# Three pairs of chunks added on VectorE ahead of the head sums in an edge-wise graph attention, with small copies moved to ScalarE

## The reference

```
def gatv2_layer(x, Ws, bs, Wd, bd, attn, src, dst):
    hs = (x @ Ws + bs).reshape(N, H, HD)              # N 1250, H 8, HD 96
    hd = (x @ Wd + bd).reshape(N, H, HD)
    hs_e = hs[src]                                    # one row per edge, sorted by dst
    e = jax.nn.leaky_relu(hs_e + hd[dst], SLOPE)
    logits = jnp.einsum('ehd,hd->eh', e, attn)        # 8 logits per edge
    m = jax.ops.segment_max(logits, dst, num_segments=N)
    ex = jnp.exp(logits - m[dst])
    s = jax.ops.segment_sum(ex, dst, num_segments=N)
    alpha = ex / s[dst]
    out = jax.ops.segment_sum(alpha[..., None] * hs_e, dst, num_segments=N)
    return jax.nn.elu(out).reshape(N, DM)
x = x + gnn(layernorm(x)) + linear_attention(layernorm(x))
x = x + ffn(layernorm(x))
```

## Time and profile before

| what | kernel before |
|---|---|
| time of three executions | 2284.72 us (2283.73 to 2286.36) |
| span of the profiled execution, first to last instruction | 2282.6 us |
| PE busy | 2141.9 us, 94% |
| DVE busy | 1671.1 us, 73% |
| ACT busy | 1120.7 us, 49% |
| POOL busy | 770.2 us, 34% |
| mean granted clock of TensorE | 0.974 of full speed |
| HBM traffic | 169 GB/s over the span |

### The profile page before, as it was taken

One profiled execution on the slowest core, in us unless ns is written; L12 is line 12 of the kernel. 1 busy time (PEld: TensorE's weight loads), 2 busy tenths in 40 slices (PEclk: granted clock), 3 DMA queues, 4 the chain that ended last, 5 costly groups with the idle time before them and its releaser, 6 DMA issues. The chain is left out here.

```text
span 2282.6 us, 91572 instructions
## 1 busy us (share of the span) xinstructions
PE 2141.9 (94%) x32341; PEld 1718.3 (75%) x32342; DVE 1671.1 (73%) x4413; ACT 1120.7 (49%) x2757; POOL 770.2 (34%) x798
## 2 busy tenths in 40 slices
PE   5999999998999999999996899899999999999578
PEld 3665555555899999999995556589999999999467
DVE  5224997343888888888887674488888888888873
ACT  1101210023666666666664324466666666666463
POOL 0000001111555555555552001255555555554000
PEclk9999999999999999999998899999999999999789
DMA  5000224333788888888874024488888888887301
GB/s 190 0 1 11 76 97 101 106 121 86 239 251 250 252 250 248 247 256 252 251 249 135 23 85 131 131 244 252 251 249 252 251 252 251 250 249 225 133 22 47
DMA packets 139236, 397.61 MB, mean 174 GB/s; under 512 B 21704, under 2 KB 76267, under 8 KB 139123
## 3 DMA queue, kind: packets, MB, share of 16 engines
q0 software_dynamic: 59584, 298.64, 43.0%
q1 hardware_dynamic: 76525, 90.41, 12.6%
q10 hardware_dynamic: 3044, 7.45, 1.1%
HBM read 368.18 MB, written 16.78 MB: 169 GB/s over the span
## 5 line engine op out<-in xcount | busy, mean ns | idle before, releaser
L498 ACT ACTIVATE at_relu<-at_turned,ah_attn_size 128x512 f32<-128x512 f32 x1092 | 717.9, 694 | 432.0 <-PE at_turned L557 430.6
L479 POOL DMA_INDIRECT at_rows<-table,ah_index x360 | 361.3, 1004 | 295.3 <-DVE ah_index L681 104.1
L479 POOL DMA_INDIRECT ah_room<-table,ah_index x352 | 351.5, 998 | 291.1 <-DVE ah_index L681 122.4
L555 PE MATMUL at_turned<-ah_place,dst_rows 96*128 96x128 bf16 x2208 | 401.1, 223 | 19.3 <-ACTq L533 9.6
L557 PE MATMUL at_turned<-ident,ah_room 128*128 128x128 f32 x2208 | 416.4, 279 | 0.0
L557 PE MATMUL at_turned<-ident,at_rows 128*128 128x128 f32 x2160 | 403.6, 277 | 0.5 <-issue 0.4
L555 PE MATMUL at_turned<-at_place,dst_rows 96*128 96x128 bf16 x2160 | 388.9, 222 | 0.0
L677 DVE SCALAR_TENSOR_TENSOR sums<-sums,at_factor,at_total 128x97 f32 x1456 | 344.0, 310 | 9.0 <-issue 5.1
L557 PEld LDWEIGHTS at_turned<-ident,ah_room 128*128 128x128 f32 x2208 | 317.7, 144 | 24.8
L557 PEld LDWEIGHTS at_turned<-ident,at_rows 128*128 128x128 f32 x2160 | 308.0, 143 | 23.2 <-issue 0.6
L667 DVE TENSOR_TENSOR at_spread<-at_lined,at_weight 128x1024 f32<-128x1024 f32 x182 | 223.0, 1225 | 131.4 <-ACT at_weight L508 118.0
(11 more groups left out here) (318 smaller groups left out, 3195.8 us busy)
## 6 DMA issues: line engine op xcount, KB each, us to landing
at_flags<-run_flags SPq DMA_DIRECT2D x182, 64.0 KB
dst_rows<-pr_parts SPq DMA_DIRECT2D x76, 144.0 KB, 2.5
ah_place<-local_rows SPq DMA_DIRECT2D x92, 96.0 KB
at_place<-local_rows SPq DMA_DIRECT2D x90, 96.0 KB
table<-ah_room SPq DMA_DIRECT2D x20, 400.0 KB, 2.4
ah_room<-table,ah_index POOLq DMA_INDIRECT x368
at_rows<-table,ah_index POOLq DMA_INDIRECT x360
mx_w<-in_L_mix_W_qkv SPq DMA_DIRECT2D x2, 2304.0 KB, 19.3
```

The source lines that it names most:

```text
L479: pool.indirect_dma_start(rows[b][:, j, :], None, table, bass.IndirectOffsetOnAxis(index[b][:, j:j + 1], 0)).then_inc(gathered[b], 16)
L498: act.activation(relu[c][:], turned[chunk(b, c)][:], ACT.Relu, scale=attn_size[:, c:c + 1]).then_inc(bent, 1)
L555: pe.matmul(into, dst_rows[:, bass.ds(at[j], 1), c * P:(c + 1) * P].rearrange("p o d -> p (o d)"), place[b][:, j * P:(j + 1) * P], start=T ...
```

## The change

Four edits inside attend:

- Chunks 4 and 5 are no longer summed alone: DVE adds chunk 4 to 5 as a third join, and sum_heads has three groups of four matmuls in place of four. The first join (0 into 1) is issued a slot earlier, in the slot in which the macro tile is turned, ahead of spread_out. The other two stand at the top of the next slot, where both joins stood before.
- line_up and the multiplication of spread_out become one scalar_tensor_tensor for each of the four groups (is_equal, then mult), 128x256 each, on DVE. at_lined goes. messages waits for two of the four pieces before its first pair and for all four before its second.
- copy_index goes from DVE to ACT, between the bends of chunks 0 and 1. gather gets a wait for the additions of the macro tile four earlier.
- first_maximum goes. ACT copies one column of at_right into at_maxima (128x91) in drops; DVE adds still_first and takes the maximum once, at the end of a layer. The semaphore raised now counts two increments a slot (RISES), scanned three, and drops waits for both of its predecessors on ACT.

On DVE, in the slot behind the main loop (in the loop the order is the same, with register instructions between, and with at_place ahead of the last piece), the rows before are these. Relu1 to relu5 are the chunks; sums is add_total.

The diff, without the declarations of tiles and the list of semaphore names:

```
@@ -347,3 +347,4 @@
 BANKS = 4
-SCANS = 4
+SCANS = 3
+RISES = 2
 ADDS = 2 * G
@@ -351,3 +352,3 @@
 TAIL = 3
-JOINED, ALONE = ((0, 1), (2, 3)), (4, 5)
+JOINED = ((0, 1), (2, 3), (4, 5))
 LOOPS = (NM - TAIL) // UNROLL
@@ -469,2 +470,4 @@
                 def gather(m, b, paced=True):
+                    if paced:
+                        pool.wait_ge(added, (m - UNROLL) * ADDS + 2 * ADDS)
                     pool.wait_ge(index_ready, m + 1)
@@ -474,3 +477,3 @@
                         if paced and j == 2:
-                            pool.wait_ge(spread_ready, m - 2)
+                            pool.wait_ge(spread_ready, (m - 3) * G + G)
                         if paced and j == 3:
@@ -502,3 +505,4 @@
                     act.activation(rise[:], left[(b + 1) % 2][:, P - 1:P], ACT.Identity, bias=right[:, 0:1], scale=-1.0).then_inc(raised, 1)
-                    act.wait_ge(raised, m + 2)
+                    act.activation(maxima[:, bass.ds(m, 1)], right[:, 0:1], ACT.Copy).then_inc(raised, 1)
+                    act.wait_ge(raised, m * RISES + (RISES + 1))
                     act.activation(drop[:], quarter_mask[:, 0], ACT.Relu, scale=rise[:]).then_inc(dropped, 1)
@@ -516,5 +520,10 @@
-                def slot(turn, head, first=False, fresh=False):
+                def copy_index(m, b):
+                    act.activation(index[b][:], rows_of(src_index, m), ACT.Copy).then_inc(index_ready, 1)
+
+                def slot(turn, head, message=None, first=False):
                     if turn:
                         bend(turn[0], turn[1], 0, first)
+                        if message:
+                            copy_index(message[0] + UNROLL, message[1])
                         bend(turn[0], turn[1], 1, first)
@@ -537,3 +546,3 @@
                     for b in range(UNROLL):
-                        slot(macro(i, b + 2), macro(i, b + 1))
+                        slot(macro(i, b + 2), macro(i, b + 1), macro(i, b))
                 slot(macro(LOOPS, 2), macro(LOOPS, 1))
@@ -565,6 +574,2 @@
                         pe.matmul(head_row(j), rows[b][:, j, D + 1::QUAD], ident[:], start=True, stop=False)
-                    for c in ALONE:
-                        pe.wait_ge(bent, m * KC + (BANKS + c + 1))
-                        for j in range(G):
-                            pe.matmul(head_row(j), sign_mask[:, c, :], relu[c][:, j * P:(j + 1) * P], start=False, stop=False)
                     for k, (_, c) in enumerate(JOINED):
@@ -586,3 +591,5 @@
                     if pair == 0:
-                        pe.wait_ge(spread_ready, m + 1)
+                        pe.wait_ge(spread_ready, m * G + G // 2)
+                    else:
+                        pe.wait_ge(spread_ready, m * G + G)
                     pe.wait_ge(added, m * ADDS + (pair + 1) * ADDS // 2)
@@ -634,10 +641,4 @@
-                def line_up(m, fresh):
-                    if not fresh:
-                        dve.wait_ge(spread_ready, m)
-                    dve.tensor_tensor(lined[:], over(iota_row[:, 0:S], G),
-                                      rows_of(dst_local, m).unsqueeze(2).broadcast_to([P, G, S]), ALU.is_equal).then_inc(lined_ready, 1)
-
-                def join(m):
-                    for from_, c in JOINED:
+                def join(m, pairs):
+                    for from_, c in pairs:
                         dve.wait_ge(bent, m * KC + (BANKS + c + 1))
@@ -647,3 +648,3 @@
                     dve.wait_ge(heads_done, m + 1)
-                    dve.wait_ge(raised, m + 1)
+                    dve.wait_ge(raised, m * RISES + RISES)
                     dve.wait_ge(flags_loaded[b], 16 * (round + 1))
@@ -660,10 +661,8 @@
-                def first_maximum(m):
-                    dve.scalar_tensor_tensor(first_max[:], right[:, 0:1], still_first[:, bass.ds(m, 1)], first_max[:], ALU.add, ALU.max).then_inc(scanned, 1)
-
                 def spread_out(m, b):
-                    dve.wait_ge(lined_ready, m + 1)
                     dve.wait_ge(weights_ready, m * EXPS + (EXPS + 1))
-                    dve.tensor_tensor(spread[:], lined[:].unsqueeze(2).broadcast_to([P, G, H, S]),
-                                      weight[:].rearrange("p (j h) -> p j h", j=G).unsqueeze(3).broadcast_to([P, G, H, S]), ALU.mult).then_inc(spread_ready, 1)
+                    for j in range(G):
+                        dve.scalar_tensor_tensor(spread[:, j], over(iota_row[:, 0:S], H), dst_local[:, bass.ds(m, 1), j:j + 1].rearrange("p o j -> p (o j)"),
+                                                 weight[:, j * H:(j + 1) * H].unsqueeze(2).broadcast_to([P, H, S]),
+                                                 ALU.is_equal, ALU.mult).then_inc(spread_ready, 1)
@@ -679,6 +678,3 @@
-                def copy_index(m, b):
-                    dve.tensor_copy(index[b][:], rows_of(src_index, m)).then_inc(index_ready, 1)
-
-                def slot(head, message, after=None, fresh=False, more=False):
+                def slot(head, message, after=None, turn=None):
                     if message:
@@ -686,4 +682,3 @@
                     if head:
-                        line_up(head[0], fresh)
-                        join(head[0])
+                        join(head[0], JOINED[1:])
                     if message:
@@ -691,4 +686,2 @@
                             add_total(message[0], message[1], j, at)
-                    if more:
-                        copy_index(message[0] + UNROLL, message[1])
                     if head:
@@ -697,5 +690,6 @@
                         shift(head[0])
-                        first_maximum(head[0])
                     if after:
                         build_place(*after)
+                    if turn:
+                        join(turn[0], JOINED[0:1])
                     if head:
@@ -705,6 +699,5 @@
                 dve.memset(left[1][:], -FAR).then_inc(cleared, 1)
-                dve.memset(first_max[:], -FAR).then_inc(cleared, 1)
-                dve.wait_ge(cleared, 3)
+                dve.wait_ge(cleared, 2)
                 dve.sem_inc(scanned, SCANS)
-                dve.sem_inc(raised, 1)
+                dve.sem_inc(raised, RISES)
                 step = Link(dve, firsts)
@@ -714,8 +707,8 @@
                 step(dve.tensor_scalar(single[:], single[:], -FAR, None, ALU.mult))
-                slot(None, None, macro(0, 2))
-                slot(macro(0, 0), None, None, fresh=True)
+                slot(None, None, macro(0, 2), macro(0, 0))
+                slot(macro(0, 0), None, None, macro(0, 1))
                 with dve.Fori(0, LOOPS) as i:
                     for b in range(UNROLL):
-                        slot(macro(i, b + 1), macro(i, b), macro(i, b + 3), more=True)
-                slot(macro(LOOPS, 1), macro(LOOPS, 0))
+                        slot(macro(i, b + 1), macro(i, b), macro(i, b + 3), macro(i, b + 2))
+                slot(macro(LOOPS, 1), macro(LOOPS, 0), None, macro(LOOPS, 2))
                 slot(macro(LOOPS, 2), macro(LOOPS, 1))
@@ -732,2 +725,5 @@
                     step(dve.tensor_tensor(known[there], reached[there], cont[there], ALU.add))
+                dve.wait_ge(raised, NM * RISES + RISES)
+                step(dve.tensor_tensor(maxima[:], maxima[:], still_first[:], ALU.add))
+                step(dve.tensor_reduce(first_max[:], maxima[:], AX.X, ALU.max))
                 step(dve.tensor_tensor(apart[:], known[:], first_max[:], ALU.subtract))
```

More of the change, by code:

```diff
@@ L374 @@
 AT_SIGNALS = ("cleared", "index_ready", "index_seen", "place_ready", "turned_done", "bent", "heads_done", "scanned", "raised", "dropped",
-              "turned_back", "weights_ready", "lined_ready", "spread_ready", "totalled", "added", "firsts", "merge_ready", "merged",
+              "turned_back", "weights_ready", "spread_ready", "totalled", "added", "firsts", "merge_ready", "merged",
               "merge_seen", "joined")
@@ L414, in attend @@
         rise, drop, first_max = sb("at_rise", [P, 1]), sb("at_drop", [P, G * HH]), sb("at_first_max", [P, 1])
+        maxima = sb("at_maxima", [P, NM])
         weight = sb("at_weight", [P, G * H])
         factor = [sb(f"at_factor{b}", [P, G, HH]) for b in range(2)]
-        lined = sb("at_lined", [P, G, S])
         spread = sb("at_spread", [P, G, H, S])
@@ L427, in attend @@
         (cleared, index_ready, index_seen, place_ready, turned_done, bent, heads_done, scanned, raised, dropped, turned_back, weights_ready,
-         lined_ready, spread_ready, totalled, added, firsts, merge_ready, merged, merge_seen, joined) = sems[0:len(AT_SIGNALS)]
+         spread_ready, totalled, added, firsts, merge_ready, merged, merge_seen, joined) = sems[0:len(AT_SIGNALS)]
         local_loaded, flags_loaded, gathered = (
```

## The result

The changed kernel takes 2338.64 us (2336.55 to 2341.51, four runs) against 2285.54 us (2283.73 to 2287.12) before: a ratio of 1.0233 with an interval of 1.0219 to 1.0248. It is 2.3% slower. 2333 us with a range of 2296 to 2360 was forecast. The profiled span went from 2282.6 to 2336.7 us.

The account below looks back on a forecast made before the run. PE's queue bound the kernel at 7.185 us a slot; a ring of waits through the third join would make it 7.45, 0.265 more times 182 slots, 48 us, plus 1 us for layers' ends: 2333 us, range 2296 to 2360.

Parts of the forecast that it names:

- Chunk 4 seen 1.75 us after at_back's load: From PE's weight load of at_back until ACT sees chunk 4 turned: 1.75 us, ends 1.70 and 1.81.
- The ring: Slot's loop of waits, at_back, chunk 4, bends, join into relu5, additions, scans, shift: 7.42 us, 7.37 to 7.48; chance 0.74.
- The loop's turn, 7.55: Slot at the loop's turn: PE's extra 0.26 us hides in the ring (7.42) or adds (7.68); 7.55 taken.
- DVE's sum 6.79: DVE's work in a new slot without waits: 6.79 us, under PE's 6.90, so not the bound.
- Four pieces 1.57: New spreading on DVE, four scalar_tensor_tensor of 256 elements: 0.39 us each, 1.57 us, hidden by the ring.
- PE falls to some 46.5 of 50 us: PE's busy time in the loop stretch falls from 49.63 to some 46.5 of 50 us.
- 1 us for the layers' ends: Two small DVE instructions added at each layer's end: about 0.5 us a layer, 1 us for two.
- The two copies 0.2 each: ACT's copies for at_index and at_maxima: 0.2 us each, just fitting under the ring with 0.05 us to spare.
- PE stays the bound: Rival: PE's queue bounds, four fewer matmuls give 6.90 us a slot, 2245 us; chance 0.13.
- Gain and wait cancel: Rival: a ring of 7.1 to 7.2 us cancels PE's gain, 2280 to 2300 us; chance 0.08.
- The spreading is the bound: Rival: four DVE pieces cost over 2.20 us; at 0.66 each, 2413 us; chance 0.05.
- The four matmuls cost nothing: Rival: dropping them saves PE nothing, it needs 7.12 us, the ring's 7.42 stands; included in the ring's 0.74.

Follow-up runs that it names:

- The two chained ones: Changed kernel with joined chunk 3 added into chunk 4, chunk 5 alone: 2283.57 us; the same with at_index's copy first and at_place between the dependent joins: 2289.99 us.
- the last kernel: Changed kernel with chunk 4 added into chunk 1, chunk 5 alone, at_index's copy first, at_lined separate and one spreading multiplication: 2264.61 us, 0.9908 of the kernel before.

## Why the prediction was right

Each step, by its term:

- **Chunk 4 seen 1.75 us after at_back's load:** 1.78, inside 1.70 to 1.81. **Bend 4 0.57, factors 0.58, bend 5 and hand-over 0.77, join 0.66:** 0.59, 0.58, 0.75, 0.67. **Additions 1.81, scans 0.96:** 1.80, 0.97. **Shift 0.32:** 0.35 from shift's start to at_back's load; its hand-over had been borrowed from ACT and DVE, and the one to PE is 0.06. The ring is 7.49 and 7.42 was forecast, from 7.37 to 7.48: the terms were each within 0.03, but their errors mostly add up, and the ring lies just above its stated end.
- **The loop's turn, 7.55:** too high. Six slots in a row lasted 7.52, 7.48, 7.48, 7.49, 7.48 and 7.48 us, turn included. PE's extra stand ahead of the messages there (0.51 us, put down to "issue") hides in the ring. This error and the last one have opposite signs, so part of the nearness of 2333 to 2338.64 us is luck: an average of 7.49 instead of 7.45 over the stretch, and 7.512 over a layer.
- **DVE's sum 6.79:** the waits take 0.57 of 7.48, so 6.91. Most of the 0.12 is the join ahead of the wait, which counts with its whole duration, 0.74 and not 0.66, since the next instruction waits beyond its end; the rest is in the other joins (0.67) and at_place (0.28). **Four pieces 1.57:** 812.40 - 810.82 = 1.58; the straight line between the two neighbouring sizes held. Hidden, as the third join undone shows.
- **DVE waits 0.63 ahead of the join, PE 0.52 ahead of at_back:** 0.57 and 0.50, at these places.
- **PE falls to some 46.5 of 50 us:** a miss, it is 47.77. The 0.50 us is the stand of the weight loads. The matmuls before them run on, and PE itself is idle for only 0.33 us at a time there (6.5 us in 20 waits from 700 to 900 us). The forecast took the loads' stand for PE's idle time; the forecast of the time does not hang on it.
- **The first gather at 2.5 us into the turn:** 2.48 (809.91, with PE turning from 807.43), and hidden, as the third join undone shows.
- **1 us for the layers' ends:** the two instructions and the dearer spreading make VectorE's way from the last left scan to the next additions 0.96 us longer, 7.00 us against 6.04. Between the layers nothing of it is left, behind the second 0.8 us.
- **The two copies 0.2 each:** 0.11 and 0.12, hidden. The Trainium skill (VectorE: DVE Perf Modes, The TRN2 errata) gives 224 cycles plus the elements at 1.2 GHz, an estimate of 0.19 us. The rows have durations of 0.19 for both, so the trace agrees for the duration, while the distance to the next start, which is what ScalarE's queue pays, is shorter.

The rivals fell one by one. "PE stays the bound": PE is 47.77 of 50 us busy. "Gain and wait cancel": the slot is 7.49 and not 7.1 to 7.2. "The spreading is the bound": spare work beside it is free. "The four matmuls cost nothing": three groups of loads take 0.66 us, 0.22 each, the figure of the earlier trace rows; and of the four kernels that drop four matmuls without a join that waits for bend 5, the two with chunk 4 added into chunk 1 beat the one before by 17 and 20 us, about half of 0.22 x 182 = 40. The two chained ones do not. The follow-ups show where such a sum fails: the join amid the additions had a second consumer, the additions a second operand when the factors moved, and the chains two joins of which one reads the other's result.

## What to carry to other kernels

When a vector instruction on an engine with an in-order queue gets a new operand, add up the whole way that comes back to it (who makes the operand, who queues behind the instruction, who waits for those) before counting what the change takes from the busiest engine: here 0.22 us less work on TensorE became 0.30 us more in each of 182 slots, and no engine was full afterwards. A spare instruction on either side of the suspected wait tells a ring from a full engine in two runs. To use the saving, give the join operands that are already there: chunk 4 into the sum made a slot earlier, and the last chunk alone, with at_index's copy first on ScalarE, was 0.8 to 0.9% faster than before. And go through every consumer of what is moved: the join amid the additions was expected at 2293 us and took 2417.82, for the one consumer left out.

## What the runs showed of the hardware

- Two 128x128 additions on VectorE, the second waiting for the first by a semaphore, last 0.60 us as a pair in the trace and cost 0.54 on the way of the ring: the next instruction starts before the last has ended.
- Two VectorE instructions of 128x512 of which the second reads the first's result, with a semaphore between, last 1.53 to 1.60 us together, 0.12 to 0.19 more than independent ones (1.41).
- In these traces VectorE's additions begin no sooner than 1.26 us after TensorE's first weight load for their totals (1.28 with the third join undone and with it amid the additions, 1.26 and 1.27 in the last kernel). I had taken 0.94.
- The kernel before took 2572 us on one chip and 2284 to 2286 on the others. It was not profiled on the slow one; the two variants that were moved 191 to 212 GB/s in the loop there, against 252 and 253 on a chip of the others. Ratios between chips are not to be compared, and here not even their signs.
